# Reciprocal roots of the low-rank rows: from three Newton steps on VectorE to an exponent and one step on GpSimd, with a new order of parts, in a two-layer decoder kernel

## The reference

```python
def rms_norm(x, w):
    return x * jax.lax.rsqrt(jnp.mean(x * x, axis=-1, keepdims=True) + EPS) * w
...
q = rms_norm(hidden_states @ q_a_w, q_a_ln_w) @ q_b_w            # rank 192, then 32 heads of 128 + 64
q_pass, q_rot = (q[..., :DN], q[..., DN:])
ckv = hidden_states @ kv_a_w
c_kv, k_rot = (ckv[..., :KVLR], ckv[..., KVLR:])                 # 64 latent columns, 64 rotated ones
kv = rms_norm(c_kv, kv_a_ln_w) @ kv_b_w
...
x = _layernorm(x + _L0_attn_ref(...))    # latent attention, 32 heads
x = _layernorm(x + _L0_xattn_ref(...))   # learned adjacency over the context
x = _layernorm(x + _L0_ffn_ref(...))     # 7 routed experts and a shared one, top 2
x = _layernorm(x + _L1_attn_ref(...))    # attention, 16 heads of 16
x = _layernorm(x + _L1_xattn_ref(...))   # bilinear attention with the context
x = _layernorm(x + _L1_ffn_ref(...))     # gated feed-forward, hidden 1024
```

## Time and profile before

| | before |
|---|---|
| median of 3 runs | 714.95 us (713.79 to 715.62) |
| the profiled execution's own time | 713.86 us |
| its span, first to last instruction | 712.0 us |
| granted TensorE clock, mean | 0.995 |
| PE busy | 686.8 us (96%) |
| DVE busy | 539.4 us (76%) |
| ACT busy | 496.5 us (70%) |
| POOL busy | 389.1 us (55%) |

### The profile page before, as it was taken

How to read it: one execution, slowest core, us unless ns; L and a number is a source line. 1 busy time by engine, 2 the same in 40 slices (tenths; PEclk the granted TensorE clock), 3 DMA queues, 4 the chain that set the end, 5 groups by cost and what they waited for, 6 DMA issues and landing times.

```text
span 712.0 us, 14718 instructions
## 1 busy us (share of the span) xinstructions
PE 686.8 (96%) x4886; PEld 576.6 (81%) x4886; DVE 539.4 (76%) x1701; ACT 496.5 (70%) x1277; POOL 389.1 (55%) x647
## 2 busy tenths in 40 slices
PE   8899999999999999999987999999989999999995
PEld 6577898889888888889875988888967777768885
DVE  4967899887788969888878956566788778749464
ACT  4787865888568684888877867665756676876641
POOL 4269642885267731878965546834781321336652
PEclk9999999999999999999999999999999999999998
DMA  8671001140431302212021002210120000010301
GB/s 286 172 227 34 16 1 45 46 120 1 124 114 37 114 2 65 54 33 61 1 90 46 1 0 90 77 58 1 45 89 3 4 2 4 3 46 1 122 27 45
DMA packets 34419, 41.06 MB, mean 58 GB/s; under 512 B 6620, under 2 KB 27238, under 8 KB 34344
## 3 DMA queue, kind: packets, MB, share of 16 engines
q1 hardware_dynamic: 33800, 39.80, 19.0%
q10 hardware_dynamic: 544, 0.33, 0.1%
HBM read 30.02 MB, written 1.05 MB: 44 GB/s over the span
## 4 chain that ended last, share of the span: by engine, by line
PE 82%; DVE 8%; POOL 3%; issue 2%; SPq 2%; ACT 1%; DMA 1%; POOLq 0%; DVEq 0%
PE bank L1181 72%; PE bank L1195 10%; SPq L2625 1%; DVE top_tok L2258 1%; DVE router_buf L1891 1%; POOL w_split_lo L2361 1%; POOL probs L2361 1%; POOL stat L2361 1%; DMA qT<-xT_plain 1%; DVE y L1894 1%; POOL qT L2361 0%; ACT x L1593 0%; DVE bn L1926 0%; DVE key_tok L1894 0%; DVE xT_lo L1894 0%
## 5 line engine op out<-in xcount | busy, mean ns | idle before, releaser
L2358 POOL TENSOR_SCALAR probs<-probs,soft 128x256 f32<-128x256 f32 (+1 forms) x256 | 105.7, 437 | 51.3 <-DVE soft L2054 49.8
L1681 ACT ACTIVATE probs<-probs,soft 128x256 f32<-128x256 f32 (+1 forms) x256 | 113.0, 447 | 15.1 <-DVE soft L2046 14.7
L1181 PE MATMUL bank<-xT_hi,w_split_hi 128*128 128x512 f32 x256 | 104.0, 406 | 2.5 <-POOL w_split_lo L2361 1.4
L2361 POOL TENSOR_TENSOR w_split_lo<-w_raw,w_split_hi 128x512 fp32r<-128x512 f32 (+2 forms) x57 | 73.0, 1289 | 52.3 <-ACT w_split_hi L1586 48.3
L1181 PE MATMUL bank<-xT_lo,w_split_hi 128*128 128x512 f32 x256 | 100.6, 393 | 0.0
L2046 DVE CUSTOM_DVE_ANT_0 probs<-bank,mask 128x256 f32<-128x256 f32 (+1 forms) x256 | 78.8, 353 | 25.6 <-PE bank L1181 23.7
L1181 PE MATMUL bank<-keyT,qT 128*128 128x256 f32 (+1 forms) x512 | 93.5, 330 | 2.7 <-POOL qT L2361 2.7
L1181 PEld LDWEIGHTS bank<-keyT,qT 128*128 128x128 f32 x512 | 81.9, 190 | 14.7 <-POOL qT L2361 4.8
L2361 POOL TENSOR_TENSOR qT<-qT,xT_plain 64x512 f32<-64x512 f32 x44 | 56.0, 1273 | 53.8 <-DMA qT<-xT_plain 51.6
L1181 PE MATMUL bank<-xT_hi,w_split_lo 128*128 128x512 f32 x192 | 75.7, 394 | 0.0
L1586 ACT ACTIVATE qT<-bank 64x512 f32<-64x512 f32 (+1 forms) x80 | 47.3, 593 | 29.7 <-PE bank L1181 26.3
(11 more groups left out here) (245 smaller groups left out, 1814.5 us busy)
## 6 DMA issues: line engine op xcount, KB each, us to landing
qT<-xT_plain SPq DMA_DIRECT2D x88, 64.0 KB, 2.0
w_raw<-in_w_nopeT SPq DMA_DIRECT2D x8, 512.0 KB, 3.7
w_raw_heads<-in_w_o SPq DMA_DIRECT2D x8, 512.0 KB, 5.4
qT<-rope_buf SPq DMA_DIRECT2D x40, 64.0 KB, 2.0
w_raw<-in_w_gateT SPq DMA_DIRECT2D x8, 256.0 KB, 2.7
w_raw<-in_w_upT SPq DMA_DIRECT2D x8, 256.0 KB, 3.1
w_raw<-in_w_downT SPq DMA_DIRECT2D x8, 256.0 KB, 3.7
w_raw<-in_L_ffn_Wup SPq DMA_DIRECT2D x7, 256.0 KB, 2.7
```

What stands on the lines that cost most here:

```text
L1181: return t.matmul(out, lhsT, rhs, start=start, stop=stop, skip_group_check=shared)
L1681: ins = s.activation(p[:, at], p[:, at], ACT.Exp, bias=st[:, 0, r:r + 1], scale=-1.0, accum_out=st[:, 1, r:r + 1])
L2358: return g_.tensor_scalar(out, in0, s1, s2, op0, op1)
L2361: return g_.tensor_tensor(out, in0, in1, op)
```

## The change

`down_root` has a part on POOL now. On DVE only the addition of epsilon stays, one instruction of 128 x 8, which signals `low_seeded`; the integer seed and the three Newton steps (11 further instructions of 128 x 8) are gone. POOL raises the sums to the power of -0.5 and does one Newton step, five instructions. `power` grows from 4 to 8 columns. Two signals of the last layer norm are merged into the general ones; what waits for what stays the same there. URGENT is replaced as a whole (a few lines of each stand below), and in NEAR the window of POOL goes from 0.3 to 0.5 and that of SP from 0.5 to 0.3.

```diff
-    NEAR = {"PE": 0.0, "ACT": 0.3, "DVE": 0.3, "POOL": 0.3, "SP": 0.5, "DMA": 0.05, "WAY": 0.0}
+    NEAR = {"PE": 0.0, "ACT": 0.3, "DVE": 0.3, "POOL": 0.5, "SP": 0.3, "DMA": 0.05, "WAY": 0.0}
     URGENT = {
-        ("adj_T", 0): -24, ("adj_mask", 2): 70, ("adj_mask", 3, 1): 17, ("adj_sim", 2): 45, ("adj_top", 1): 362,
+        ("adj_top", 1): 254, ("adj_top", 3): 67, ("att_norm", 0): 136, ("att_norm", 1): 38, ("att_norm", 2): -16,
...
-        stage(("down_root", h), "DVE 2.7", ("down", h))
+        stage(("down_root", h), "DVE 0.2, POOL 2.2", ("down", h), ("zero",))
...
-    power = sb("power", [P, TH])
+    power = sb("power", [P, 2 * TH])
...
             elif name == "down_root":
                 h, = k
                 place = in_stat.place["down", h]
-                ve, r, s_ = (stat[place][:, j, 0:2 * TH] for j in range(3))
                 w.wait_ge(*low_squared[tiles_of[h][-2]])
                 w.wait_ge(*own.now)
-                own(seed(ve, r, sums[:, h, :, :].rearrange("p a t -> p (a t)"), 1e-6))
-                newton_steps(ve, r, s_).then_inc(low_rsqrt.sem, 1)
+                ts(stat[place][:, 0, :], sums[:, h, :, :].rearrange("p a t -> p (a t)"), 1e-6, None, ALU.add).then_inc(low_seeded.sem, 1)
...
+        def newton_step(r, s, ve):
+            w.wait_ge(*own.now)
+            own(tt(s, r, r, ALU.mult))
+            w.wait_ge(*own.now)
+            own(tt(s, s, ve, ALU.mult))
+            w.wait_ge(*own.now)
+            own(ts(s, s, -0.5, 1.5, ALU.mult, ALU.add))
+            w.wait_ge(*own.now)
+            return tt(r, r, s, ALU.mult)
...
+            elif name == "down_root":
+                h, = k
+                ve, r, s_ = (stat[in_stat.place["down", h]][:, j, :] for j in range(3))
+                w.wait_ge(*zeroed["zero"])
+                w.wait_ge(*low_seeded[h])
+                own(tt(r, ve, power[:, :], ALU.pow))
+                newton_step(r, s_, ve).then_inc(low_rsqrt.sem, 1)
```

More of the change, by code:

```diff
@@ L12 @@
 U32 = mybir.dt.uint32
-I32 = mybir.dt.int32
 ALU = mybir.AluOpType
@@ L72 @@
 SCALE1 = float(HD1) ** -0.5
-RSQRT_SEED, NEWTON_STEPS = float(0x5F3759DF), 3
 U_EXPERT, U_QKV, U_FFN = NG, NG + NE, NG + NE + 1
@@ new lines @@
+        ("f_up", 1, 1): 51, ("ffn_norm", 3): 5, "ffn_norm": 51, ("load", "xT2"): -24, ("load", 21): 51,
+        ("load", 24): -121, "load": 29, ("mix_norm", 1): 142, ("norm", 0, 5, 0): -21, ("norm", 1): -33,
+        ("norm", 1, 2, 0): -8, ("norm", 1, 3, 0): 14, ("norm", 1, 5, 1): 13, ("norm", 2): -56, ("norm", 2, 0, 0): 31,
+        ("norm", 2, 1, 1): 8, ("norm", 3): -78, ("norm", 3, 0, 1): -102, ("norm", 3, 2, 0): 14, ("norm", 3, 5, 0): 19,
+        ("norm", 3, 6, 0): -14, "norm": 176, ("out", 0): -50, ("out", 0, 5): -1, ("out", 0, 6): 38, ("out", 0, 7): 125,
@@ L770, in write_program, with parts_of_statistics @@
     names = []
+    def parts_of_statistics(step):
+        return ["first tile", step] if step == ("out_stats", B - 1) else [step]
     def signal(name, keys):
@@ L876, in write_program @@
     low_odd = signal("low_odd", [t for h, in keys("down") for t in tiles_of[h][1::2]])
-    low_rsqrt = signal("low_rsqrt", [h for h, in keys("down_root")])
+    low_seeded, low_rsqrt = (signal(name, [h for h, in keys("down_root")]) for name in ("low_seeded", "low_rsqrt"))
     key_lat = signal("key_lat", [t for h, in keys("down_scale") for t in tiles_of[h]])
@@ L893, in write_program @@
     xT_lo = signal("xT_lo", keys("xT"))
-    seeded = signal("seeded", [s for s in ORDER["DVE"] if s in in_stat.place and s[0] != "down"])
-    last_seeded = signal("last_seeded", [0])
+    seeded = signal("seeded", [part for s in ORDER["DVE"] if s in in_stat.place and s[0] != "down" for part in parts_of_statistics(s)])
     out_normed = signal("out_normed", keys("out_norm", range(TB)))
@@ L924, in write_program @@
     normed = signal("normed", heads(keys, "norm"))
-    newton = signal("newton", [s for s in ORDER["POOL"] if s in seeded.at])
+    newton = signal("newton", [part for s in ORDER["POOL"] if s in seeded.at for part in parts_of_statistics(s)])
     unit_set = signal("unit_set", [0])
-    last_newton = signal("last_newton", [0])
     zeroed = signal("zeroed", [s[0] for s in ORDER["POOL"] if s[0] in ("zero", "rows1")])
@@ L1930, in statistics @@
             w.wait_ge(*own.now)
-            ve, r, s = (stat[place][:, j, 0:len(tiles)] for j in range(3))
-            variance = bn[place][:, 0:len(tiles), 7]
-            if step in seeded.at:
-                ts(ve, variance, eps, None, ALU.add).then_inc(seeded.sem, 1)
-            else:
-                own(seed(ve, r, variance, eps))
-                own(newton_steps(ve, r, s))
+            ts(stat[place][:, 0, 0:len(tiles)], bn[place][:, 0:len(tiles), 7], eps, None, ALU.add).then_inc(seeded.sem, 1)
         def last_added(ins):
@@ L1953, in last_statistics @@
             w.wait_ge(*own.now)
-            ts(stat[place][:, 0, i:i + 1], bn[place][:, i, 7:8], LN_EPS, None, ALU.add).then_inc((last_seeded if i == 0 else seeded).sem, 1)
+            ts(stat[place][:, 0, i:i + 1], bn[place][:, i, 7:8], LN_EPS, None, ALU.add).then_inc(seeded.sem, 1)
         def batch_rows(t, b):
@@ L2366, in reciprocal_root @@
             if step == ("out_stats", B - 1):
-                w.wait_ge(*last_seeded[0])
-                root(step, 0, 1).then_inc(last_newton.sem, 1)
+                w.wait_ge(*seeded["first tile"])
+                root(step, 0, 1).then_inc(newton.sem, 1)
                 w.wait_ge(*seeded[step])
```

94 lines of the change are left out of this document (31 added, 63 removed), and 40 rows, old and new, of the table URGENT.

## The result

The changed kernel takes 706.89 us (median of four runs, 704.91 to 708.59), the kernel before beside it 714.37 us (713.26 to 715.62). The ratio is 0.9894, with a 95% interval from 0.9862 to 0.9926: 7.5 us or 1.1% faster. The profiled execution took 706.38 us, of which 704.4 are its span; 713.86 and 712.0 stood there before.

What follows compares the result with a forecast made beforehand. PE's matmul stream, busy 96% of the span, was taken as the bound. Gains of 0.8 + 1.7 = 2.5 us off 713.86 gave 711.4, or 712.5 for the median; stated forecast 712.1 us, range 708.0 to 717.3.

Steps and rivals of the forecast that it cites:

- The root's engine move is worth 0: Opening: root on POOL takes 2.75 us and ends at 14.9, formerly 14.93; worth 0, 0.7 us either way.
- DVE's relief counts only as far as PE waits for it: Opening: DVE is relieved of 5.0 us, counting only where PE waits for what stood behind the roots.
- First step q at 23.8, first scores at 36.8, gain 0.8: Opening on PE: step q 2.1 us earlier, scores at 36.8 instead of 37.59 us; gain 0.8 us (0 to 1.4).
- The halt of 1.70 us at 56.29 goes, and nothing is late next: PE's wait for `qT`: swaps issued 4 us or more earlier, gain 1.7 us (0 to 1.7); the next step q costs 0.
- new halt for `qT` between 44 and 55 us: Sign against the forecast, in the opening: PE waiting anew for `qT` there.
- The opening gives 2.5 us: Sum of the opening's two gains, 0.8 + 1.7 us, taken off the profiled execution's 713.86 us.
- The rest of the program trades like for like: Behind the opening: other moves gain nothing; lists around the 383.65 us halt read the same, halts from 510 to 640 left.
- The statement on 60 to 340 us: PE is busy for 279.76 of 280 us there, so nothing is to be had.
- Would make it wrong as a whole: PE's idle time from 60 us on changes by more than 2 us: Sign, behind the opening: such a change in PE's idle time makes the whole forecast wrong.
- Faster by more: Rival, chance 0.08: routing chain hidden, no halt and no half clock (2.6 + 1.7 us) besides the 2.5: 708.2 us.
- 714.4 in one rival: No change that counts: later stages give back 2 us of the opening's gain; chance 0.29 with its other form.
- 714.1 in another: Power costs 1 us more, twice, on POOL; step q 2 us later, 0.8 becomes -1.2; shares 0.29 with no change.

Runs made afterwards that it cites:

- `move_only`: Changed kernel's code with every engine's list in the old order, root on POOL just ahead of its scaling: 714.20 us against 713.77 before, ratio 0.9998.
- `order_only`: Code of before (root on DVE with three Newton steps) with all lists in the new order: 707.09 us against 713.77 before, ratio 0.9883.
- `after_again`: The changed kernel itself, unaltered, run again on the chip of later runs: 706.31 us, ratio 0.9894 to the kernel before.
- `new_to_69us`: Changed kernel with lists in the new order up to some 69 us and the old order from there: 713.89 us, ratio 0.9992 to before.
- `new_to_150us`: Changed kernel with lists in the new order up to some 150 us and the old order from there: 713.98 us, ratio 0.9993 to before.
- `rows_first`: Changed kernel with DVE's xT_lo of the experts' last token tile moved ahead of the first routing gate: 705.49 us, ratio 0.9867 to before.
- `new_to_400us`: Changed kernel with lists in the new order up to some 400 us and the old order from there: 710.72 us, ratio 0.9938 to before.
- `weights_first`: Changed kernel with POOL's w_split_lo of head group 0 moved ahead of the second half's root: 707.94 us, ratio 0.9899 to before.

## Why the prediction was wrong

*The root's engine move is worth 0.* Right within what the interval of `move_only` tells (0.9998, 0.2% either way). The prediction had given it 0.7 us either way, and in the one trace of it PE is 0.6 us behind at the first scores. The power was costed at 1.65 us and took 1.65 and 1.85, the root 2.75 and took 2.78. The ratio of the Trainium skill ("GPSIMD Engine Reference", section 3.1), by which it would take 0.5 us more, does not hold at this width: the Newton instructions of 128x8 took 0.20 to 0.21 us each on POOL, against 0.17 on DVE.

*DVE's relief counts only as far as PE waits for it.* Right: `order_only` keeps DVE's 11 instructions for each root and is as fast.

*First step q at 23.8, first scores at 36.8, gain 0.8.* The mechanism was right, the size off. The weights ended at 24.56 instead of 23.7, since the first root started at 12.82 and not at 12.17: in this execution the clock first rose to full at 8.0 us, in that of before at 5.2. The halt of 1.82 us ahead of the step leaves room for a fall of the clock, which was not costed, and it fell. The scores started at 38.27, 0.7 us later than before. Where it held, they started at 35.5 to 36.2 us, earlier than forecast.

*The halt of 1.70 us at 56.29 goes, and nothing is late next.* The first half was right. For the second, the "new halt for `qT` between 44 and 55 us" that the prediction named as a sign against it stands in every trace with the new opening in which the clock held up to there, with 0.6 to 2.3 us, and in `after_again`, where it fell, with 1.0 us. In the profile of after it is not seen; there the first scores came later, at 38.27 us.

*The opening gives 2.5 us.* In the trace of after it gave 1.7 by the 479th matmul, on the mean of nine traces 1.3, and on the medians of `new_to_69us` and `new_to_150us` nothing that can be told.

*The rest of the program trades like for like.* **This is the step that failed**, and it holds nearly the whole gain: 3 to 4 us between 150 and 400 us and about 3 behind 510. The prediction had compared the lists around the largest halt, found them alike, and took that for the rest. But PE's waits of 1.3, 0.7, 0.7 and 0.6 us were in the view of the waits, in stages that lacked 6.2 and 4.7 us of PE. Each is small; together with the shorter wait for `q_rows` they are 3.8 us. The statement on 60 to 340 us holds: PE's busy time there is 279.76 and 279.68 us, and between the 479th and the 2277th matmul the two traces need the same time within 0.2 us.

*Would make it wrong as a whole: PE's idle time from 60 us on changes by more than 2 us.* It fell from 18.7 to 15.0 us. These 3.7 us are not the whole: by the matmuls the changed kernel gains 5.6 us from 341 us on, so some 2 us of its gain lie where the trace counts PE as busy.

*The rivals.* "Faster by more" came true, at 706.9 instead of 708.2, but not by its mechanism: the routing chain it rested on stands unchanged, 2.59 and 2.57 us. `rows_first`, which takes that halt away, gained nothing that its interval tells, though its trace gains 2.2 us in that stage.

*The sums.* The working ends at 712.5 us and the forecast is 712.1, for which no reason is given; and the same rest of 0.5 us gives 714.4 in one rival and 714.1 in another. Neither slip decides anything here.

*What stays open.* Of the 3 to 4 us between 150 and 400 us, 2.2 stand in the traces. Some 0.8 us may be the clock (at half speed `new_to_150us` spends 4.4 us more than before on its chip, `new_to_400us` 2.7), and no trace says why. The rest is within what the intervals leave. Why PE's busy stretches get shorter by some 2 us was not looked into, and a seam inside the second attention was not tried.

## What to carry to other kernels

Where a bound engine is at 97%, add up all of its waits over half a us, not the largest alone: here the waits that went away or grew shorter, by 0.5 to 1.3 us each, gave more together than the one of 1.7 us on which most of the forecast rested. Compare two traces at matmuls up to which both have issued the same work, not at a time or at the n-th of one kind. When a change carries a new order with it, time the two apart first; two kernels settled it. A halt taken away is worth its length only if nothing is 1 to 2 us behind it, and in this opening something was each time: `key_tok` and the load of `ctxT`, or the swaps.

## What the runs showed of the hardware

Whether the clock falls behind a halt of under 2 us differs between executions of the same lists. The halt of 1.81 to 1.82 us before the first step q stands in ten traces; in four the clock went to 0.5 (1.2 GHz) behind it for 3.41 us, in six it did not. It need not be chance: in the four the clock had first risen to full (2.4 GHz) at 6.8 to 8.2 us, in the six at 5.2 to 6.5 us. No run varies that alone. Behind the halt of 1.6 to 1.7 us for `q_rows` it fell in two traces (`new_to_69us`, `new_to_400us`) and not in three. Behind that of 2.5 to 2.6 us in the routing it fell in all eleven that have it. Behind the 1.28 us for `ctxT` in `weights_first` it fell as well. Span and granted clock go together between the executions of one kernel: of the 24 executions of before, the eight at a granted clock of 0.997 spanned 710.3 to 711.4 us, the one at 0.990 spanned 716.5. A difference of 2 us between two profiled executions says nothing before their clocks are compared.

And a halt can hide another: at half clock PE reaches the next wait later and finds it shorter or over (for `qT` at 46 us, 2.2 us in `rows_first`, 1.0 in `after_again`, none in after). The same holds for the reading of a profile after a change, in which a wait that is not seen is not yet gone.
